# A ViT tower on one core: patch embedding in three full token tiles a pair of images, the last five tokens of all images embedded ahead of the loop

## The reference, cut to what matters

```
tokens = einsum('npd,hd->nph', patches(x), W) + b        # 64 x 196 x 768 by 768 x 192
h = concat([class_token, tokens]) + pos_embed            # 64 x 197 x 192
h = h + attention_0(layernorm(h))   # 64 query tokens, 133 keys, one head, projection
h = h + mlp_0(layernorm(h))
h = h + attention_1(layernorm(h))   # 12 heads of 64
h = h + mlp_1(layernorm(h))         # quantised
```

## Time and profile before

| | |
|---|---|
| median of three runs | 2365.83 us |
| the profiled execution: its own time | 2370.66 us |
| its span | 2368.9 us |
| PE busy over the span | 2161.4 us (91%) |
| first stage (embedding and attention_0) | to about 364 us |
| embedding matmuls (L477) | 2304 |
| granted TensorE clock, mean | 0.989 |

### The profile page before, as it was taken

The page is one execution under the profiler, slowest core; times in us unless marked ns, Lnnn a source line. Parts: engine busy times, 40 slices in busy tenths (PEclk is TensorE's granted clock), DMA queues, the critical chain, the costliest instruction groups (busy, mean ns, idle before and its releaser), DMA issues. The chain is left out here.

```text
span 2368.9 us, 76500 instructions
## 1 busy us (share of the span) xinstructions
PE 2161.4 (91%) x25422; PEld 1694.2 (72%) x25422; DVE 1996.3 (84%) x4966; ACT 2009.4 (85%) x5695; POOL 1712.6 (72%) x2215
## 2 busy tenths in 40 slices
PE   6899999999999799999999999999999999988876
PEld 5788876888777577777777777777777777765554
DVE  5777777889786789998999989999899998986997
ACT  4688876777774799999999999999999999995986
POOL 5778852333333589899998989989899898993554
PEclk9999999999999999999999999999999999998999
DMA  6344411000000376666666666666666666672111
GB/s 191 109 123 126 130 34 29 6 5 35 15 13 6 60 124 122 121 119 123 120 123 121 119 123 120 123 121 119 123 119 125 120 120 123 118 128 43 56 46 61
DMA packets 734156, 222.65 MB, mean 94 GB/s; under 512 B 667590, under 2 KB 732720, under 8 KB 733808
## 3 DMA queue, kind: packets, MB, share of 16 engines
q1 hardware_dynamic: 733776, 221.36, 45.9%
q10 hardware_dynamic: 288, 0.20, 0.0%
HBM read 46.49 MB, written 9.68 MB: 24 GB/s over the span
## 5 line engine op out<-in xcount | busy, mean ns | idle before, releaser
L1524 POOL TENSOR_TENSOR b_pr<-b_pr,fc 128x394 f32<-128x394 f32 (+1 forms) x768 | 652.0, 870 | 124.0 <-DVE fc L1444 124.0
L1373 ACT ACTIVATE b_pr<-b_scores,fc 128x197 f32<-128x197 f32 (+1 forms) x1536 | 632.1, 440 | 2.6 <-issue 1.2
L1509 POOL TENSOR_TENSOR b_halves<-b_pr,b_halves 128x394 f16<-128x394 f32 (+1 forms) x640 | 564.9, 908 | 31.9 <-ACT b_halves L1342 27.7
L1281 PE MATMUL b_banks<-fp,wqkv 128*128 128x197 f16 x3840 | 377.7, 249 | 42.8 <-DVE b_qk L1428 38.8
L1438 DVE TENSOR_REDUCE fc<-b_scores 128x2 f32<-128x394 f32 x768 | 395.7, 556 | 3.5 <-PE b_scores L1299 1.4
L1281 PEld LDWEIGHTS b_banks<-fp,wqkv 128*128 128x128 f16 x3840 | 320.0, 98 | 83.9 <-DVE b_qk L1428 60.6
L1342 ACT ACTIVATE b_halves<-b_pr 128x788 f16<-128x788 f32 x384 | 342.8, 893 | 4.5 <-POOL b_pr L1524 3.5
L1373 ACT ACTIVATION_READ_ACCUMULATOR b_pr<-b_scores,fc 128x1 f32 (+1 forms) x1536 | 341.0, 222 | 0.0
L985 POOL TENSOR_TENSOR h<-h,fp_bias 69x192 f32 (+3 forms) x128 | 133.4, 1069 | 266.9 <-DVE m_xn L139 266.9
L1428 DVE SCALAR_TENSOR_TENSOR b_qk<-b_banks,b_qk 128x394 f16<-128x394 f32 x384 | 214.9, 560 | 101.7 <-ACT b_qk L1356 101.5
L1288 PE MATMUL b_banks<-wqkv,fp 128*128 128x384 f16 (+1 forms) x1280 | 254.6, 330 | 40.7 <-DVE h L1463 38.8
(11 more groups left out here) (252 smaller groups left out, 4378.5 us busy)
## 6 DMA issues: line engine op xcount, KB each, us to landing
patches<-in_x SPq DMA_DIRECT2D x64, 588.0 KB, 4.3
b_pt<-b_halves SPq DMA_TRANSPOSE x384, 3.1
out<-z_res SPq DMA_DIRECT2D x62, 96.0 KB
fc<-b_halves SPq DMA_TRANSPOSE x192, 3.2
fp<-b_halves SPq DMA_TRANSPOSE x192, 3.2
m_raw_weights<-in_wqkv SPq DMA_DIRECT2D x2, 1152.0 KB, 6.9
out<-z_res SPq DMA_DIRECT2D x32, 51.8 KB
h<-h SPq DMA_DIRECT2D x32, 44.2 KB
```

The source lines that it names most:

```text
L1281: last = t.matmul(out[:, g * SEQ:(g + 1) * SEQ], w[:, (2 * n + g) * P:(2 * n + g + 1) * P], x, start=(j == 0), stop=(j == 4))
L1373: last = nc.scalar.activation(pr[n % 3][0:ROWS[c], c, e, :], scores[n % 2][0:ROWS[c], e, c * SEQ:(c + 1) * SEQ], ACT.Exp, bias=nmx[n % 2][ ...
L1509: nc.gpsimd.tensor_tensor(halves[n % 3][0:ROWS[c], c, 1, :, 0:SEQ], pr[n % 3][0:ROWS[c], c], halves[n % 3][0:ROWS[c], c, 0, :, 0:SEQ], ALU ...
L1524: last = nc.gpsimd.tensor_tensor(p, p, inv, ALU.mult)
```

## The change

- **Three tiles a pair.** The class column and the first 191 patch tokens make 192 columns an image (`MAIN`), laid out by the host, so a pair has 384 columns, three full tiles of 128. `E0` is now 18 matmuls, `E1` is 36: the second tile of image 1, and one tile that holds the last 64 columns of both images. For odd images the host rotates the columns, so that the shared tile is contiguous.
- **The last five tokens** (`LATE`) of all 64 images, 320 columns, are loaded at the start (`x_late`, with tables `pos_late` and `cls_late`), split by ACT and DVE, and embedded in tiles of 125, 125 and 70 tokens by 54 matmuls ahead of the loop. DVE adds their table and writes `late_res`. PE's first `E0` and `E1` wait for that (`late_added`), since the products use the same PSUM tiles. SP then moves five rows an image from `late_res` into `h` with small transfers (two a pair), and both `b0` and `b1` wait for them (`late_moved`). SP's second pair of patches stands behind its wait for `late_added`.
- **Buffers.** `parts` has one buffer a pair of images and two of them, in place of one an image, so ACT `h` waits for the products of the pair two back.
- **Adds.** `a0` is one add in place of two, `a1` is three in place of two (two of 64 rows).
- **DVE's list.** `b0` moves from behind `p^^^^` to the head of the next round: `b0^ b1^ r^ ... a0 p^^^^ o^^^^^ t^^^^ a1`. The lists of PE, ACT and POOL are as before.

```diff
@@ constants and orders
+LATE = SEQ - P - NQ
+MAIN = SEQ - LATE
+LATE_IMAGES = P // LATE
-    DVE_ORDER = ("b1^ r^ i^^^^^ ... x^^^ a0 p^^^^ b0 o^^^^^ t^^^^ a1").split()
+    DVE_ORDER = ("b0^ b1^ r^ i^^^^^ ... x^^^ a0 p^^^^ o^^^^^ t^^^^ a1").split()
-        patches = [sb(f"patches{q}", [P, PATCH_K, SEQ]) for q in range(4)]
-        parts = [sb(f"parts{m}", [P, 2, PATCH_K, SEQ + 1], F16) for m in range(2)]
+        patches = [sb(f"patches{q}", [P, PATCH_K, MAIN]) for q in range(4)]
+        parts = [S["wqkv"]...[:, 0:size].rearrange("p (a k t) -> p a k t", a=2, k=PATCH_K),
+                 sb("parts1", [P, 2, PATCH_K, 2 * MAIN], F16)]
@@ SP
-                        sp.dma_start(patches[2 * b + m][:, :, 1:SEQ], A["x"][2 * p + m]).then_inc(loaded[2 * b + m], 16)
+                        sp.dma_start(patches[2 * b + m][:], A["x"][2 * p + m]).then_inc(loaded[2 * b + m], 16)
+                    if p == 0:
+                        sp.wait_ge(late_added, 1)
+                    if p > 1:
+                        sp.wait_ge(counted[0], p - 1)
+                    for i in (2 * p, 2 * p + 1):
+                        row = LATE * (i % LATE_IMAGES)
+                        sp.dma_start(h[NQ:NQ + LATE, i, 1, :], late_res[row:row + LATE, i // LATE_IMAGES, :]).then_inc(late_moved[b], 16)
@@ ACT, step h
-                        if later(p):
-                            act.wait_ge(made[m], p)
-                        copy(parts[m][:, 0, :, 0:SEQ], patches[2 * b + m][:]).then_inc(patch_hi[m], 1)
+                        if later(p - 1):
+                            act.wait_ge(made[1], p - 1)
+                        copy(parts[b][:, 0, :, m * MAIN:(m + 1) * MAIN], patches[2 * b + m][:]).then_inc(patch_hi[m], 1)
@@ PE, step E
-                        for k in range(PATCH_K):
-                            for n, (pa, pb) in enumerate(PARTS):
-                                last = product(1, k, pa, pb, start=(k == 0 and n == 0), stop=(k == PATCH_K - 1 and n == 2))
+                        if m == 1:
+                            for k in range(PATCH_K):
+                                for n, (pa, pb) in enumerate(PARTS):
+                                    last = t.matmul(tokens[1][:, D:2 * D], parts[b][:, pa, k, P:2 * P], tok_w[:, pb, k, :],
+                                                    start=(k == 0 and n == 0), stop=(k == PATCH_K - 1 and n == 2))
@@ PE, ahead of the rounds
+                pe.wait_ge(late_split, 1)
+                for n, rows in enumerate(late_tiles):
+                    first = LATE * LATE_IMAGES * n
+                    for k in range(PATCH_K):
+                        for j, (pa, pb) in enumerate(PARTS):
+                            last = t.matmul(tokens[n // 2][0:rows, (n % 2) * D:(n % 2 + 1) * D], late_parts[:, pa, k, first:first + rows],
+                                            tok_w[:, pb, k, :], start=(k == 0 and j == 0), stop=(k == PATCH_K - 1 and j == 2))
+                last.then_inc(late_made, 1)
@@ DVE, steps a and b
-                        for c in range(2):
-                            last = v.tensor_tensor(h[0:ROWS[c], 2 * p + n, c, :], tokens[n][0:ROWS[c], c * D:(c + 1) * D],
-                                                   posb[0:ROWS[c], c, :], ALU.add)
+                        last = v.tensor_tensor(h[:, 2 * p + n, 0, :], tokens[n][:, 0:D], posb[:, 0, :], ALU.add)
+                        if n == 1:
+                            for m in range(2):
+                                last = v.tensor_tensor(h[0:NQ, 2 * p + m, 1, :], tokens[1][own(m), D:2 * D], posb[0:NQ, 1, :], ALU.add)
-                        dve.wait_ge(taken[n], p + 1)
+                        dve.wait_ge(taken[1], p + 1)
+                        dve.wait_ge(late_moved[b], 16 * p + 32 - 16 * b)
@@ DVE, ahead of the rounds
+                dve.wait_ge(late_hi, 1)
+                v.tensor_tensor(late_parts[:, 1], r_late, late_parts[:, 0], ALU.subtract).then_inc(late_split, 1)
+                then(v.tensor_tensor(late_pos, late_pos, late_cls, ALU.add))
...
+                dve.wait_ge(late_made, 1)
+                for n, rows in enumerate(late_tiles):
+                    last = v.tensor_tensor(late_res[0:rows, n, :], tokens[n // 2][0:rows, (n % 2) * D:(n % 2 + 1) * D], late_pos[0:rows], ALU.add)
+                last.then_inc(late_added, 1)
```

More of the change, by code:

```diff
@@ L233, in embed_attend @@
         cls_b = front[:, PATCH_K * D:(PATCH_K + 2) * D].rearrange("p (c d) -> p c d", c=2)
+        late = n_img * LATE
+        late_tiles = [LATE * len(range(k, min(k + LATE_IMAGES, n_img))) for k in range(0, n_img, LATE_IMAGES)]
+        assert len(late_tiles) <= 4
+        at = (PATCH_K + 2) * D
+        r_late = front[:, at:at + PATCH_K * late].rearrange("p (k t) -> p k t", k=PATCH_K)
+        at += PATCH_K * late
+        late_parts = front[:, at:at + PATCH_K * late].bitcast(F16).rearrange("p (a k t) -> p a k t", a=2, k=PATCH_K)
+        at += PATCH_K * late
+        late_pos, late_cls = (front[0:LATE * LATE_IMAGES, at + k * D:at + (k + 1) * D] for k in range(2))
+        late_res = S["wo"][:].rearrange("p a f d -> p (a f d)")[:, 0:2 * D * len(late_tiles)].bitcast(F32).rearrange("p (n d) -> p n d", d=D)
         tok_w = sb("tok_w", [P, 2, PATCH_K, D], F16)
@@ L317, in _ @@
                     sp.dma_start(dst, src).then_inc(tok_loaded, 16)
-                rounds(sp, ["d"], count, load, {"d": {1: load_masks, 3: load_quantised}}, first=3)
+                for dst, src in late_loads:
+                    sp.dma_start(dst, src).then_inc(late_loaded, 16)
+                rounds(sp, ["d"], count, load, {"d": {1: load_masks, 3: load_quantised}}, first=count)
             @block.gpsimd
             def _(pool):
-                for q in range(4):
-                    last = nc.gpsimd.memset(patches[q][:, :, 0:1], 0.0)
-                last.then_inc(zeroed, 1)
                 g = nc.gpsimd
@@ L448, in _ @@
                 copy(tok_w[:, 0], r_tok).then_inc(tok_hi, 1)
+                act.wait_ge(late_loaded, 16 * len(late_loads))
+                copy(late_parts[:, 0], r_late).then_inc(late_hi, 1)
                 copy(S["pw"][:, 0], r_pw[:])
@@ L474, in job, with product @@
                             pe.wait_ge(taken[m], p)
-                        def product(c, k, pa, pb, **flags):
-                            return t.matmul(tokens[m][0:ROWS[c], c * D:(c + 1) * D], parts[m][:, pa, k, COLS[c]], tok_w[:, pb, k, :], **flags)
+                        else:
+                            pe.wait_ge(late_added, 1)
+                        lo = m * 2 * P
+                        def product(k, pa, pb, **flags):
+                            return t.matmul(tokens[m][:, 0:D], parts[b][:, pa, k, lo:lo + P], tok_w[:, pb, k, :], **flags)
                         for k in range(PATCH_K):
                             for pb in range(2):
-                                product(0, k, 0, pb, start=(k == 0 and pb == 0), stop=False)
+                                product(k, 0, pb, start=(k == 0 and pb == 0), stop=False)
                         for k in range(PATCH_K):
@@ L484, in job @@
                                 pe.wait_ge(patch_split[m], PIECES * p + k // 2 + 1)
[L485 to L488 removed]
+                            last = product(k, 1, 0, start=False, stop=(k == PATCH_K - 1))
+                        if m == 1:
[3 more added lines that the diff above has]
+                                                    start=(k == 0 and n == 0), stop=(k == PATCH_K - 1 and n == 2))
                         last.then_inc(made[m], 1)
@@ L1808, in laid_out @@
     qk = qkv[:, 0:2].reshape(D, 2, PAIRS, P).transpose(0, 2, 1, 3).reshape(D, 2 * HID)
+    patches = x.reshape(n, 3, npat, 2, 8, npat, 16).transpose(0, 4, 6, 1, 3, 2, 5).reshape(n, P, PATCH_K, npat * npat)
+    tokens = np.concatenate([np.zeros((n, P, PATCH_K, 1), np.float32), patches[:, :, :, 0:MAIN - 1]], axis=3)
+    tokens[1::2] = np.roll(tokens[1::2], MAIN - P, axis=3)
     cls_bias = np.concatenate([f["L0_tok_class_token"].reshape(1, D), rows(f["L0_tok_b"], SEQ - 1)], axis=0)
@@ L1811, in laid_out @@
     return {
-        "x": x.reshape(n, 3, npat, 2, 8, npat, 16).transpose(0, 4, 6, 1, 3, 2, 5).reshape(n, P, PATCH_K, npat * npat),
+        "x": tokens,
+        "x_late": patches[:, :, :, MAIN - 1:].transpose(1, 2, 0, 3).reshape(P, PATCH_K, n * LATE),
+        "pos_late": np.tile(f["L0_tok_pos_embed"][MAIN:], (LATE_IMAGES, 1)),
+        "cls_late": rows(f["L0_tok_b"], LATE * LATE_IMAGES),
         "tok_w": f["L0_tok_W"].reshape(D, 3, 2, 8, 16).transpose(3, 4, 1, 2, 0).reshape(P, PATCH_K, D),
```

19 lines of the change are left out of this document (11 added, 8 removed).

## The result

The changed kernel takes 2388.55 us (median of four runs, 2386.81 to 2394.74); the kernel before, now with four runs, 2366.86. The ratio is 1.0091, interval 1.0079 to 1.0104: slower by 21.7 us. I had forecast slower by 10, at most 2387. The profiled execution took 2387.48 us, its span 2385.7. All times in the tables are in us.

A forecast was written before the change was run, and what follows sets the result against it. PE was taken to bound the steady rounds; a loop through POOL, ACT and DVE would bound next. Terms +12.0 - 4.2 + 1.9 + 0.3 = +10.0 us on 2365.8 gave 2376 us, 8-in-10 range 2356 to 2387.

The forecast's parts named there:

- Rounds with units: Pairs 2 to 10, where DVE has extra weight work behind `a1`: periods shorter, -4.2 us in sum.
- ACT's line: In pairs 2 to 10, ACT's steps `n` to `g` set when `o` begins: 7.21 us after POOL's chain ends.
- the start: Before the first `q1`: late tokens, their 54 products and pair 1's later load delay it, +12 us, bounds 8 to 15.
- the steady rounds: Ten two-pair periods from pair 10 to 30: 19.29 us each in place of 19.10, +1.9 us in sum.
- the ring: Loop of waits from POOL's chain through ACT `n` to `g` and DVE `o` to `r`, back to `q1`: 19.29 us.
- the entry through PE: Path by POOL's splits and PE's products and `t` to `a1`: 14.3 + 0.9 us after `q1`, against 15.6 for `o`.
- POOL's floor: Rival: steady period falls to POOL's own work, 17.3 us; -10 us, 2356 us in all; chance 0.11.
- PE's whole gain: Rival: steady period falls to PE's 16.1 us; -22 us, 2344 us in all; chance 0.05.
- The start was not absorbed: Rival: start costs +5 in place of +12, about 2369 us; chance 0.18, shared with slightly better steady periods.
- The clock: Rival: PE's waits drop its clock to 1.2 GHz half the time, ten periods 49 us longer, 2425 us; chance 0.04.

The follow-up runs named there:

- e6: Changed kernel with DVE's nine units of weight work placed behind `r` in place of `a1`; ratio 1.0046 to the kernel before.
- e9: Kernel before with DVE's nine units of weight work placed behind `r` in place of `a1`; ratio 0.9972 to the kernel before.
- e15: Changed kernel with POOL's splits cut to 8 columns in place of 192; one run, five periods 94.01 us, steady period 18.45 us.
- e7: Changed kernel with 8 to 46 unused filler products on PE ahead of its wait for `l12` in pairs 2, 4, 6 and 10; ratio 1.0083.
- e2: Changed kernel with ACT `h` waiting as before the change, for the products of the pair before; ratio 1.0086 to the kernel before.
- e8: Kernel before with two buffers of `parts`, no product removed; ratio 1.0052 to the kernel before.
- e5: Kernel before with the change's DVE list alone, `b0` at the head of the next round; ratio 1.0031 to the kernel before.
- e4: Changed kernel with POOL's split `l12` moved out of the chain, ahead of `q1`; 2384.5 us, ratio 1.0082 to the kernel before.
- e3: Changed kernel with 18 more products, read by nothing, in PE's first embedding group of every pair; ratio 1.0139 to the kernel before.
- e11: Changed kernel with `l12` ahead of `q1` and twelve unused filler products a period in PE's waits for splits; 2370.2 us, ratio 1.0019.

## Why the prediction was right in direction and wrong in size

- **The failed step is "Rounds with units": -4.2 forecast, +5.8 measured in its four periods (+7.1 in the five).** Its sentence "Those 18 are gone, so ACT's line decides" put `o` 7.21 us behind the end of the chain; it came 9.45, 11.89 and 8.95 us behind it, and DVE's list, with the unit in it, decided in the worst of the three. The step said of a unit only that it is on the path in both kernels, and priced none anew. The runs show three things in its place. (1) The units stand between `a1` and `r`, so `q1`, or `m` and with it `e`, waits for them, and they are stretched more than before by POOL's splits beside them: placed behind `r` they give back 11.9 us in the changed kernel and 5.2 in the kernel before (e6, e9), and without long splits they are short (e15). (2) The waits of 3 to 4 us for `l12` bring PE to its lower clock: filler gives 4.6 us (e7). (3) ACT's earlier `h` sets when POOL splits: the old wait gives 4.0 us (e2), the buffers alone cost 3.2 in the kernel before (e8). These overlap and don't add up; how much of each there is in the 7.1 stays open, and so does what the moved `b0` adds to the time (e5). Even with units off the path the five periods are 103.9 us, against 103.51 in the kernel before: the forecast gain was not there.
- **The range.** It let the start and the steady rounds grow (2376 + 3 + 7 = 2386 us, I wrote 2387) and held the rounds with units at -4.2, so it had no room for the term that failed.
- **The start, +12 forecast, +14.1 measured.** Right in mechanism. That the first loop product came at the forecast time is partly luck, as two misses cancelled. I had read 0.16 us a product over 6 us off the start of the kernel before, where POOL's splits, for which these products wait, ran beside them until 18.4 us. After, 9 products went by from 17.5 to 19 us, which is 0.16 us each, but 33 from 21 to 23.7 us, which is 0.08. Of the 2.1 us that were short, 0.8 are in the landing of pair 1 and 0.95 in the first unit, which with small splits takes 1.52 us in place of 4.07 (e15).
- **Steady rounds.** 19.29 forecast, 19.17 measured, clock 1.00, PE 86%: right, and e4 and e15 bear out the ring by taking one member from it or shortening it. Wrong in it was that the entry through PE comes 0.4 us earlier than the end of `o` (14.3 + 0.9 against 15.6 us); it is 0.2 us later, by the wait of 0.19 us at `t`. A third entry, from `s` over DVE's `m`, `x`, `a0` and `p`, was not in it at all: it is level with `g` and bounds e3.
- **Rivals.** POOL's floor and PE's whole gain did not come (POOL idles 1.5 us before `q1`). The start was not absorbed. The clock stayed at 1.00 in the steady rounds, but fell in the rounds with units and in e4. I had read the earlier trace rows, PE at 84% and 1.00, as speaking for all stretches at that share; the rows of after (75% and 0.81, 86% and 1.00) and e4 (91% and 0.93) show that the share does not decide it. The Trainium skill's rule (TensorE: Matmul & The Clock Gate, section on a second failure mode), short idling between groups of products makes the clock swing, agrees with e11 and with the six long periods of e4, not with its three short ones nor with the changed kernel's own steady rounds.
- **The rule that I should have weighed.** The Trainium skill (SBUF — State Buffer, section "Who interferes with whom") says that a DVE operation with two SBUF inputs, or in a two-port mode, and a POOL operation that reads SBUF shut each other out for a whole instruction, and that which is issued first decides who waits. The rows agree: at 86 us DVE was fast (1.65 us for six) and one split of POOL took 2.52 us, at 104 us POOL was fast and DVE late. Which of the two was issued first at 86 us the rows don't show, as both start within 0.1 us.

## What to carry to other kernels

Before you credit a shorter path, list what else runs in the moved window on an engine that shares something with it, and price it anew: a DVE operation of 0.21 us took 0.83 beside a row of POOL's splits. Put work that nothing waits for behind the result that the other engine waits for, not in front of it. And compare a change with a before that has the same good lists: here two edits of lists gave the old kernel as much as the change with all its repairs.
